# A ring of 24 normalised tiles, first loads on two queues, and a later wait for attention's last store

## The reference, cut to what matters

```python
x = L0_attn_a_x
x = x + _L0_attn_a_ref(_layernorm(x), Wq, Wk, Wv, Wo)          # causal, 16 heads of 16
x = x + _L0_ffn_ref(_layernorm(x), norm_scale, gate_w, gate_b, mlp1_w, mlp1_b, mlp2_w, mlp2_b)
x = x + _L0_attn_b_ref(_layernorm(x), w_qkv, w_fc, b_fc, gamma, beta)
x = x + _L0_ffn_ref(_layernorm(x), ...)                        # the same weights again
...
def _L0_ffn_ref(x, norm_scale, ...):
    ms = jnp.mean(x * x, axis=-1, keepdims=True)
    t = (x * jax.lax.rsqrt(ms + EPS) * norm_scale).reshape(Bx * Sx, Dx)
    y = _moe(t, gate_w, gate_b, ...)                           # each row by its best 2 of 8 experts
    return x + y.reshape(Bx, Sx, Dx)
```

## Time and profile before

| | |
|---|---|
| median of 3 runs | 1771.57 us |
| lowest and highest of them | 1766.80 and 1778.27 us |
| the profiled execution, device time | 1780.99 us |
| its span | 1779.3 us |
| mean granted TensorE clock in it | 0.944 |
| `out_rows` in it, from SP's first load to the first instruction of `rank` | 583.40 to 682.5 us |

### The profile page before, as it was taken

One profiled execution on the slowest core, in us unless ns is written; L12 is line 12 of the kernel. 1 busy time (PEld: TensorE's weight loads), 2 busy tenths in 40 slices (PEclk: granted clock), 3 DMA queues, 4 the chain that ended last, 5 costly groups with the idle time before them and its releaser, 6 DMA issues. The chain is left out here.

```text
span 1779.3 us, 35884 instructions
## 1 busy us (share of the span) xinstructions
PE 1642.0 (92%) x11140; PEld 1206.5 (68%) x11141; DVE 1278.2 (72%) x2670; ACT 1048.0 (59%) x1851; POOL 796.1 (45%) x773
## 2 busy tenths in 40 slices
PE   7889999999999794999999998699975999999998
PEld 3454444444443683999999998344544999999997
DVE  5678788888882667677777776358886777777776
ACT  3336677776777443666666664546654666666664
POOL 5431112112121122666666665225542566666664
PEclk9999999999999875999999999899975999999999
DMA  4655254453531752332232222301112222222222
GB/s 138 188 142 130 86 135 111 114 131 103 121 96 49 159 184 70 86 47 48 48 49 48 48 49 36 109 1 48 48 47 82 45 47 47 47 47 47 47 47 38
DMA packets 102667, 140.85 MB, mean 79 GB/s; under 512 B 18160, under 2 KB 86768, under 8 KB 99504
## 3 DMA queue, kind: packets, MB, share of 16 engines
q1 hardware_dynamic: 65638, 90.88, 19.5%
q0 software_dynamic: 31808, 37.32, 13.0%
q10 hardware_dynamic: 5130, 11.54, 1.9%
HBM read 74.21 MB, written 56.69 MB: 74 GB/s over the span
## 5 line engine op out<-in xcount | busy, mean ns | idle before, releaser
L555 ACT ACTIVATE a_Pt<-a_p_st 128x512 f32<-128x512 f32 (+2 forms) x624 | 302.2, 592 | 132.2 <-PE a_p_st L636 131.8
L582 DVE TENSOR_REDUCE mx<-a_p_sn 128x2 f32<-128x256 f32 (+1 forms) x600 | 333.3, 627 | 63.1 <-PE a_p_sn L619 53.7
L1321 ACT COPY R<-values_then_w 128x1024 f32 x284 | 283.0, 1044 | 38.7 <-issue 21.4
L1270 PE MATMUL e_p_g<-e_tT,R 128*128 128x128 f32 x2272 | 280.5, 277 | 1.5 <-ACT e_tT L1313 1.5
L1270 PE MATMUL e_p_l<-e_tT,R 128*128 128x128 f32 x2272 | 277.8, 276 | 0.0
L1282 PE MATMUL e_p_y<-w,e_hid 128*128 x1136 | 269.6, 380 | 5.8 <-DVE e_hid L1390 5.8
L1270 PEld LDWEIGHTS e_p_g<-e_tT,R 128*128 128x128 f32 x2272 | 268.3, 194 | 2.4 <-ACT e_tT L1313 2.3
L1270 PEld LDWEIGHTS e_p_l<-e_tT,R 128*128 128x128 f32 x2272 | 266.3, 193 | 0.1
L532 POOL TENSOR_SCALAR_AFFINE_SELECT a_Pt<-a_Pt 128x512 f32<-128x512 f32 x128 | 81.5, 637 | 363.5 <-ACT a_Pt L555 363.5
L1282 PEld LDWEIGHTS e_p_y<-w,e_hid 128*128 128x128 f32 x1136 | 205.3, 191 | 28.2 <-issue 6.2
L619 PE MATMUL a_p_sn<-Kst,Qst 96*128 96x128 bf16 (+1 forms) x720 | 219.7, 332 | 1.9 <-PEq L151 1.5
(11 more groups left out here) (213 smaller groups left out, 2396.8 us busy)
## 6 DMA issues: line engine op xcount, KB each, us to landing
qk_parts<-a_part SPq DMA_DIRECT2D x64, 192.0 KB, 3.2
a_Vst<-values_then_w SPq DMA_DIRECT2D x16, 512.0 KB, 18.2
o_rows<-a_OT ACTq DMA_DIRECT2D x32, 256.0 KB, 2.8
values_then_w<-in_mlp SPq DMA_DIRECT2D x16, 512.0 KB, 4.6
t_rows<-R SPq DMA_DIRECT2D x16, 512.0 KB, 3.0
Kst<-qk_parts SPq DMA_DIRECT2D x14, 384.0 KB
Qst<-qk_parts SPq DMA_DIRECT2D x14, 384.0 KB
X<-in_x SPq DMA_DIRECT2D x8, 512.0 KB, 6.1
```

The costliest lines, as they stand in the source:

```text
L555: act.activation(weights(kb, slice(h, h + n), a, b), p_st[:, i % RING, 0:n * (b - a)].rearrange("p (n w) -> p n w", n=n), ACT.Exp, scale=D ...
L582: dve.tensor_reduce(mx[:, hs[0]:hs[-1] + 1, place], p_sn[:, (s + k) % RING, 0:w * len(hs)].rearrange("p (h w) -> p h w", w=w), AX.X, ALU.m ...
L1270: mm = pe.matmul(bank[:, s, c * P:(c + 1) * P], copied[:, s, k, at:at + P], tT[:, s, k * P:(k + 1) * P], start=(k == 0), stop=(k == KD - 1))
L1321: act.copy(copied[:, s, :, cols], g["w1"][:, bass.ds(e, 1), :, cols].rearrange("p a k n -> p (a k) n")).then_inc(copied_done, 1)
```

## The change

The ring of normalised tiles t takes places 8 to 31 of `R`, so 24 tiles in place of 8, with six semaphores `t_out`, one for each group of four. `scaled(j)` waits for a store for j from 24 on only. The second half of `OT` is now the tile `xs`, which is allocated earlier for it, and its semaphore becomes `last_out`, which outlives the phase. ACT no longer waits for the last store of that half at the end of `attend_a`; SP waits for it ahead of load 12, the first of the fourth batch, whose rows that store brings. Load 0 is issued by two engines: SP issues the values of heads 0 to 2, ACT the sums and the values of head 3. At the end of `out_rows` SP waits for six semaphores in place of two.

```diff
-    OT = mem.sb("OT", [P, 2, 512])
+    OT = [mem.sb("OT", [P, 512])[:, :], g["xs"][:, :, :].rearrange("p s d -> p (s d)")]
...
-    o_out = [mem.sem(f"o_out{c}") for c in range(2)]
+    o_out = [mem.sem("o_out0"), g["last_out"]]
...
-            for c in range(2):
-                act.wait_ge(o_out[c], 16 * U)
+            act.wait_ge(o_out[0], 16 * U)
...
-    t_out = [mem.sem(f"t_out{s}") for s in range(2)]
+    T_GROUPS = 6
+    t_out = [mem.sem(f"t_out{s}") for s in range(T_GROUPS)]
...
-        return g["R"][:, 8 + j % 8, :]
+        return g["R"][:, 8 + j % (T_GROUPS * GROUP), :]
...
+    def turned_rows_of(q):
+        b, at = 2 * q // QB, 2 * q % QB * P
+        return o_dram[b * HG:(b + 1) * HG, :, at:at + 2 * P].rearrange("u (h c) t -> h c u t", c=PAD)
+
+    def load_values(eng, q, heads):
+        for h in heads:
+            eng.dma_start(Ot[DK * h:DK * (h + 1), q % DEEP], turned_rows_of(q)[h, 0:DK]).then_inc(o_in[q % DEEP], 16)
+
+    def load_sums(eng, q):
+        eng.dma_start(Ot[DK * HG:C * HG, q % DEEP], turned_rows_of(q)[:, DK]).then_inc(o_in[q % DEEP], 16)
...
             def load(q):
                 if q >= DEEP:
                     sp.wait_ge(rows_done, 2 * (q - DEEP) + 2)
...
+                if q == NT // 2 - QB // 2:
+                    sp.wait_ge(g["last_out"], 16 * U)
+                load_values(sp, q, range(HG))
+                load_sums(sp, q)
...
                 sp.dma_start(t_dram[rows, :].rearrange("(t p) d -> p t d", p=P),
-                             g["R"][:, 8 + GROUP * (c % 2):8 + GROUP * (c % 2 + 1), :]).then_inc(t_out[c % 2], 16)
+                             g["R"][:, 8 + GROUP * (c % T_GROUPS):8 + GROUP * (c % T_GROUPS + 1), :]
+                             ).then_inc(t_out[c % T_GROUPS], 16)
...
-            load(0)
+            load_values(sp, 0, (0, 1, 2))
             sp.dma_start(wo[:, :, :], g["WoT"].rearrange("(k p) n -> p k n", p=P)).then_inc(w_in, 16)
             load(1)
...
-            for s in range(2):
-                sp.wait_ge(t_out[s], 16 * (NT // 8))
+            for s in range(T_GROUPS):
+                sp.wait_ge(t_out[s], 16 * len(range(s, NT // GROUP, T_GROUPS)))
...
+            load_sums(act, 0)
+            load_values(act, 0, (3,))
             for j in range(STEPS):
...
-                if j >= 8:
-                    dve.wait_ge(tp_done, j - 7)
-                    dve.wait_ge(t_out[j // GROUP % 2], 16 * (j // 8))
+                if j >= T_GROUPS * GROUP:
+                    dve.wait_ge(tp_done, j - T_GROUPS * GROUP + 1)
+                    dve.wait_ge(t_out[j // GROUP % T_GROUPS], 16)
...
+        g["xs"] = keep.sb("xs", [P, 2, D])
+        g["last_out"] = keep.sem("last_out")
```

More of the change, by code:

```diff
@@ L541, in copy_out @@
                     act.wait_ge(o_out[c], 16 * u)
-                act.copy(OT[:, c, :], p_o[:, c, :]).then_inc(o_copied[c], 1)
+                act.copy(OT[c], p_o[:, c, :]).then_inc(o_copied[c], 1)
             def store(u, c):
@@ L546, in store @@
                 act.dma_start(o_dram[bass.ds(u, 1), :, c * 512:(c + 1) * 512].rearrange("u p t -> (u p) t"),
-                              OT[:, c, :]).then_inc(o_out[c], 16)
+                              OT[c]).then_inc(o_out[c], 16)
             def step(u, s):
@@ L2105, in program @@
         g["R"] = keep.sb("R", [P, NT, D])
-        g["xs"] = keep.sb("xs", [P, 2, D])
         g["w2"] = keep.sb("w2", [P, E, KI, D])
```

## The result

| kernel | median of runs, us | runs | profiled execution, us | its span | its mean granted clock |
|---|---|---|---|---|---|
| before | 1771.43 (1766.8 to 1778.27) | 6 | 1780.99 | 1779.3 | 0.944 |
| changed | 1762.13 (1758.36 to 1768.19) | 6 | 1763.04 | 1761.3 | 0.952 |

The changed kernel takes 0.9957 of the time, with a 95% interval from 0.9938 to 0.9976: 7.6 us less, interval 4.3 to 11.0; the medians lie 9.3 us apart. A second series (1762.96 us in 6 runs against 1771.46 in 23) gives 0.995 (0.9935 to 0.9966). The forecast of 1760 us is 2 us too low, and the time is within its range; as a saving it was 11.8 us, where 7.6 is measured.

What follows compares the result with a forecast made beforehand. PE, busy for 92% of the span, was taken as the bound, losing time in `out_rows` to idling and half clock. From 1771.6, 7.4 (2.5 + 4.9) and 4.8 for half the clock term gave 1759.4, so 1760; range 1751 to 1773.

Steps and rivals of the forecast that it cites:

- The border: Between attention and `out_rows`: without ACT's wait for its last store, SP's first load starts 1.7 us earlier, bounds 0 and 2.25.
- Rival E: End of attention: the phase still holds until the store has landed, so 1.7 us are missing; 1761.7, chance 0.05.
- The first loads: Start of `out_rows`: issuing load 0 from SP and ACT ends its issue 0.83 us sooner, bounds 0 and 0.97.
- 3.8 behind the end of ACT's last issue: Sign at the start of `out_rows`: PE's first rows come 3.8 us behind ACT's last issue, where it was 6.3.
- The ring: Middle of `out_rows`: with 24 places the waits for stores of t go, giving PE 4.9 us, bounds 0 and 5.0.
- The clock: `out_rows` behind the third wait: the half-clock stretch goes if the pause causes it, 9.5 us or 0.
- Rival B: Same stretch of `out_rows`: the clock falls anyway; 1764.2 or 1773.7, 1767 between, chance 0.20.
- The rival drawn from it: `out_rows`: a pause of 2.14 us is too short to cause the fall, which stays; 7.4 us saved, not 16.9.
- The clock against the median: Whole kernel: the clock's gain in `out_rows` counted at half against the median run, 4.8 us.
- The sum: Whole kernel: 2.5 + 4.9 + 9.5 = 16.9 us in the trace; against the median 7.4 + 4.8, giving 1760.
- What is late next: `out_rows` after the change: SP falls behind PE by 0.5 us a group, hidden if loads land like loads.
- Rivals C and D: `out_rows`: C, `Ot` loads become the wait, 1764.3 or 1769.1, chance 0.10; D, SP's backlog delays loads, 1780.0, chance 0.05.

## Why the forecast came out, and where it did not

**The border, 1.7 us: right.** Measured 1.73 (2.25 to 0.52). The check named was 0.6 us from the end of ACT's last issue to SP's first load; it is 0.52. With the wait put back the distance is 2.23 us again, and in the kernel with the ring alone 2.27, so the wait is shown to be its cause. Rival E falls.

**The first loads, 0.83 us: wrong.** The step that failed: "That is 0.83 us by the ends, 0.97 by the beginnings; I take 0.83." From SP's first issue to PE's first rows:

| load 0 | us, one trace each |
|---|---|
| on two queues | 4.04, 3.87, 4.15, 4.21, 3.91, 4.22; 4.52 with the border's wait; 4.77 with `wo` behind load 1 |
| on SP's alone | 4.01, 3.97, 4.05 (before), 3.92, 3.99, 4.03 |

The issues end 0.8 us sooner and PE's first rows do not come sooner. There the term is at its lower bound, 0; the check "3.8 behind the end of ACT's last issue" gave 4.56, where the border alone accounts for 1.7 of the fall from 6.26. The forecast had taken PE's start to follow the last issue by a fixed 2.13 us. The traces contradict that: PE's first rows keep their distance to the first issue, which fits a transfer that is the limit, not its issue. The Trainium skill, "DMA: Bandwidth & Descriptors", section "Issuing engines are not separate DMA queues", said that issuing from several engines saves only sequencer time beside shared DMA engines; the traces agree with it. That it is the shared engines, and not something else that the split changes, was argued and not measured: from SP's first load to PE's first rows DMA's share is 0.33 in the kernel before and 0.66 in the changed one, so that in the mean the 16 engines are not full. Behind the first rows the split may still be worth something, through load 1: without the border's wait, the first turned tile came 20.84 and 20.43 us behind SP's first load with one queue, and 20.07 to 20.38 with two. Two traces do not show that this is more than scatter, since the kernel with the ring alone, on one queue, has 20.03.

**The ring, 4.9 us: right for this trace, an upper end for the kernel.** DVE's waits for the stores went, and the turns are 2.0 us apart. But the other traces with the small ring and no long fall lose 2.65 us (before again) and 3.1 us (without the ring), where the first had 4.9; DVE's waits were 5.0, 4.4, 1.9 and 1.7 us. What the ring is worth varies with these waits: 3 to 5 us.

**The clock, 9.5 us in the trace: right, with its cause shown for this stretch.** In the stage's middle, from the early rise to the steps of its end, the traces show:

| kernel | PE's longest pause there, us | clock behind it |
|---|---|---|
| before (the forecast's) | 2.14 | 0.50 for 20 us |
| before, once more | 1.65 | 0.50 for 20.5 us |
| one wait put back | 3.16 | 0.50 for 3.4 us |
| one wait put back, again | 1.86 | 0.50 for 20.5 us |
| before, another time | 1.42 | stays at 1.00 |
| without the ring | 1.18 | stays at 1.00 |
| eight others with the ring of 24 | 0.5 at most | stays at 1.00 |

Four of four traces with a pause of 1.65 us or more have the fall with it, from 0.3 us ahead of the pause's end to 1.8 us behind it, and ten of ten with shorter ones have none. The kernel with one wait put back differs from the changed one by that wait alone, so the pause is shown to bring the fall here, as far as its two traces show it. Rival B falls in this stretch.

The length of one pause is not a rule for the whole kernel, though. In the changed kernel's own trace the clock falls at the stage's end behind pauses of 1.14 and 0.94 us, and at 558.0 and 568.2, inside attention, with no pause over 0.6 us in the 6 us ahead. And it does not fall within 5 us behind a pause of 1.95 us early in the program, nor within 5 us behind one of 2.90 us near its end (the first of them, and the window behind it):

```profile
70.28 1.13 PE L358 MATMUL a_p_qk<-a_nT,a_wqkv 128*128 128x512 f32 x2 [1.95 <-DVE a_rest L303]
```

```profile
70.30:85.00 14.70, 12.49 (x58) 7.50 (x59) 10.00 (x24) 5.34 (x11) 4.72 (x4) 1.00 0.72 201
```

The Trainium skill, "TensorE: Matmul & The Clock Gate", section "HAM oscillation", shows falls behind waits of 3 to 5 us; here pauses of 1.65 to 2.14 us were enough, and the measurement decides. The rival drawn from it, with the sum at 7.4 us, is refuted by the stage of 83 us, for which it had 91 to 92.

**The clock against the median, 4.8 us: mis-sized.** This is the larger miss. "I take the clock term at half against the median" had nothing in the profile behind it. Of 51 runs of the kernel before, 6 take 1778.27 us or more, and the five of them whose clock is on record have a mean granted clock of 0.944 or 0.945; both profiles with the long fall in the stage (1780.99 and 1779.27) are among them, and the one without (1772.01, clock 0.949) is not. None of 12 runs of the changed kernel is over 1768.4. If those six are the runs with the fall, the term is worth 9.5 x 6 / 51 = 1.1 us on average. That count rests on the times and clocks of runs, of which only three have a profile, and it leaves open where in the program the other runs' clock fell.

**The sum.** With the measured terms: 1.7 for the border, 0 for the split (by PE's first rows), 3 to 4.9 for the ring, 1.1 for the clock, together about 6 to 8 us. Measured are 7.6 us (4.3 to 11.0) by the ratio. Each part alone fits as well: the ring 4.8 to 9.4 for 4 to 6, the rest 0.7 to 7.4 for 1.7. So the forecast of 11.8 us was too large by the split and most of the halved clock term, 4.5 us. The time came within 2 us of the forecast because a few us are little beside 1770, and the range, 1751 to 1773, would have held no change at all as well; the terms, and not the range, are what the runs bear out. Outside the stage, spans without the border's wait are 1678.3 us on average (seven traces, 1675.8 to 1681.9), those with it 1680.3 (five, 1678.7 to 1682.6): 2.0 us apart, of which the border is 1.7, and a scatter of 4 to 6 us within each kind, so that nothing hangs on the rest.

**What is late next: right.** SP fell behind by 0.1 and 1.4 us over two groups (8.13 and 9.37 us against 8), and no load came late enough to reach PE. Rivals C and D fall: PE has no wait for `Ot` behind 594.

**Still open.** Why the fall lasts 3.4 us in one execution and 20.5 in another of the same kernel; what beside one pause's length decides on a fall; why DVE's wait ahead of tile 16 is 2.1 us in one execution and 3.4 in another of the same kernel; what in load 0's transfer keeps PE's first rows where they are; and whether the split is worth some tenths behind them.

## What to carry to other kernels

Before a stall's side effect goes into a sum, look at more than one execution: here the profile had a fall of the clock worth 9.5 us which, by their times, 6 of 51 runs may have, and the median has nothing of it to give. A buffer that is too small costs its wait, and, where the wait idles PE (here for 1.65 us or more, though other stages had such pauses without a fall), perhaps the clock behind it; enlarge it first. Splitting the issue of a load over two queues is worth trying only where the landing follows the last issue, and a wait that is moved past the end of a block is worth what is left when the next transfer has been waited for: 1.7 us at a border whose next work does not need the data, 0.6 of 2.8 where a gather follows.

## What was not expected of the hardware

The clock, once fallen, stayed at 0.50 for 20.5 us with PE busy for all 20.50 us of them, and in another execution of the same kernel for only 3.4 us, also with PE busy throughout. PE's first rows, which wait for load 0's five DMAs, came 3.87 to 4.22 us after the first issue whether one queue issued them in 2.2 us or two in 1.4; in one trace with the border's wait it was 4.52, and in one with four more loads right behind 4.77. A gather issued 2.15 us earlier, counted from the last turned tile, took 4.59 us to PE's start in place of 3.06.
